# Issuing the loads of x and of the first three weights earlier in the sync engine's order

## The reference, cut to what matters

```
h = max(layernorm(x), 0);  x = x + L0(h, edge_weight, W_gcn, W_mlp)      # 2 rounds: A_norm @ h, @ W_gcn, @ W_mlp, leaky relu
h = max(layernorm(x), 0);  x = x + L1(h, node_vec1, ...)                 # 4 blocks of attention over edges and an MLP
h = max(layernorm(x), 0);  x = x + L2(h, W, b, diffusion_weights)        # 3 steps of adj @ cur
h = max(layernorm(x), 0);  x = x + L3(h, edge_type, basis, att, ...)     # 2 relational layers
                           # in L3: w[r] = sum_b att[r, b] * basis[b], basis is 30 x 512 x 512 per layer
```

## Time and profile before

| what | value |
|---|---|
| median of three runs | 956.01 us |
| the profiled execution | 957.61 us, of which the span from first to last instruction is 955.9 us |
| PE busy | 868.6 us (91%) |
| DVE busy | 547.2 us (57%) |
| ACT busy | 425.0 us (44%) |
| DMA, over the span | 113.27 MB, mean 118 GB/s |
| granted TensorE clock, mean | 0.957 |

### The profile page before, as it was taken

One profiled execution on the slowest core, in us unless ns is written; L12 is line 12 of the kernel. 1 busy time (PEld: TensorE's weight loads), 2 busy tenths in 40 slices (PEclk: granted clock), 3 DMA queues, 4 the chain that ended last, 5 costly groups with the idle time before them and its releaser, 6 DMA issues.

```text
span 955.9 us, 14568 instructions
## 1 busy us (share of the span) xinstructions
PE 868.6 (91%) x4318; PEld 665.3 (70%) x4319; DVE 547.2 (57%) x1212; ACT 425.0 (44%) x700; POOL 224.7 (24%) x245
## 2 busy tenths in 40 slices
PE   6999799987799998999999999999998883999998
PEld 3665565665578786787867878777876562877877
DVE  7999978566654566445674546745476657310210
ACT  4999863242247533476234762237721242030210
POOL 4000052053502235122242223341143043022200
PEclk9999999997799999999999999999999797699799
DMA  8999535433534445344462535533364660020100
GB/s 186 207 216 291 132 85 138 138 90 113 135 88 123 127 123 157 83 106 139 117 188 53 131 111 150 154 85 102 123 172 155 161 167 13 1 88 1 45 11 34
DMA packets 37801, 113.27 MB, mean 118 GB/s; under 512 B 5892, under 2 KB 6424, under 8 KB 30076
## 3 DMA queue, kind: packets, MB, share of 16 engines
q1 hardware_dynamic: 20572, 79.02, 34.4%
q10 hardware_dynamic: 17184, 33.69, 10.3%
HBM read 105.35 MB, written 7.34 MB: 118 GB/s over the span
## 4 chain that ended last, share of the span: by engine, by line
PE 43%; issue 32%; POOL 12%; DVE 9%; ACT 2%; DMA 1%; SPq 0%; DVEq 0%; POOLq 0%; ACTq 0%
PE ring L1630 25%; POOL wl L669 11%; PE ring L1732 7%; PE ring L1899 5%; PE mix_ps L1750 2%; PE ring L1648 1%; POOL rstd L674 1%; DVE stats L1087 1%; PE mix_ps L1659 1%; PE ring L1709 1%; DMA att<-in_L_gnn_att 1%; DVE y L1096 0%; DVE hb_l L1074 0%; DVE diag L1328 0%; PE ring L1807 0%
## 5 line engine op out<-in xcount | busy, mean ns | idle before, releaser
L669 POOL TENSOR_TENSOR wl<-wraw,wh 128x512 fp32r<-128x512 f32 x140 | 177.4, 1301 | 410.2 <-ACT wh L737 390.6
L1732 PE MATMUL ring<-ohs,ohd 128*128 128x512 f32 x312 | 80.1, 410 | 6.6 <-DVE ohs L1262 6.5
L1732 PEld LDWEIGHTS ring<-ohs,ohd 128*128 128x128 f32 x312 | 59.3, 195 | 31.5 <-issue 18.7
L1240 DVE SCALAR_TENSOR_TENSOR ohd<-iota,dstT,vals 128x256 fp32r x156 | 69.8, 482 | 6.0 <-issue 3.6
L737 ACT ACTIVATE wh<-wraw 128x2048 fp32r<-128x2048 f32 x35 | 66.7, 1906 | 4.9 <-DMA wraw<-in_L_gnn_root 4.9
L1074 DVE TENSOR_TENSOR qk_l<-ring,qk_h 128x512 fp32r<-128x512 f32 x32 | 21.8, 690 | 76.6 <-ACT qk_h L762 76.6
L762 ACT ACTIVATE yT_h<-ring 128x512 fp32r<-128x512 f32 x32 | 19.1, 597 | 101.5 <-PE ring L1648 101.5
L786 ACT ACTIVATE ohs<-iota,minus_srcT 128x512 fp32r<-128x512 f32 x78 | 52.3, 713 | 14.1 <-PE ring L1732 7.8
L674 POOL TENSOR_TENSOR rstd<-ve,half 128x1 f32<-128x1 f32 x48 | 27.3, 572 | 109.3 <-DVE ve L1092 109.3
L1659 PE MATMUL mix_ps<-quad,att_shift 120*32 120x512 f32 x384 | 52.2, 629 | 0.0
L1074 DVE TENSOR_TENSOR PT_l<-ring,PT_h 128x512 fp32r<-128x512 f32 x64 | 39.7, 682 | 19.6 <-ACT PT_h L762 19.6
(11 more groups left out here) (373 smaller groups left out, 2238.1 us busy)
## 6 DMA issues: line engine op xcount, KB each, us to landing
quad<-in_L_gnn_basis SPq DMA_DIRECT2D x60, 960.0 KB, 8.5
wraw<-in_L_gnn_m_w ACTq DMA_DIRECT2D x8, 1024.0 KB, 5.1
mix_scratch<-mixed SPq DMA_DIRECT2D x128, 32.0 KB, 3.7
wraw<-in_L_gnn_wv ACTq DMA_DIRECT2D x4, 1024.0 KB, 5.3
wraw<-in_L_gnn_wq ACTq DMA_DIRECT2D x4, 1024.0 KB, 5.2
wraw<-in_L_gnn_wk ACTq DMA_DIRECT2D x4, 1024.0 KB, 5.9
wraw<-in_L_gnn_wo ACTq DMA_DIRECT2D x4, 1024.0 KB, 5.4
wraw<-mix_scratch ACTq DMA_DIRECT2D x4, 1024.0 KB, 5.5
```

Source lines behind the costliest of these rows:

```text
L669: last = g.tensor_tensor(wl[s][:, k, :], wraw[s][:, k, :], wh[s][:, k, :].bitcast(F32), ALU.subtract)
L1240: return v.scalar_tensor_tensor(out, at.unsqueeze(1).broadcast_to([P, 4, HALF]), dstT[:, e], vals[:, e, :].rearrange("p a b -> p (a b)").u ...
L1732: last = te.matmul(ring[:, banks[b], :], ohd[:, s, b, :], ohs[:, s, :], start=False, stop=False)
```

## The change

The load of `x` is issued after group 6 and no longer after group 13. The loads of w0, w1 and w2 are issued after groups 8, 10 and 12 and no longer all three after group 15. Sizes, targets, semaphores and all that the other engines do stay the same.

```
             for g in range(GROUPS, EARLY_SETS * GROUPS):
                 if g < PASS_GROUPS:
                     load_pass_group(g // GROUPS, g % GROUPS)
-                    if g == PASS_GROUPS - 3:
+                    if g == GROUPS + 2:
                         sp.dma_start(x[:], rows(x_d)).then_inc(x_loaded, 16)
-                    elif g == PASS_GROUPS - 1:
-                        for w in range(3):
-                            sp.dma_start(wraw[slot(w)][:], weight_source(w)).then_inc(weight_loaded[slot(w)], 16)
+                    elif g in (8, 10, 12):
+                        w = (g - 8) // 2
+                        sp.dma_start(wraw[slot(w)][:], weight_source(w)).then_inc(weight_loaded[slot(w)], 16)
                 else:
                     load_group(g // GROUPS, g % GROUPS)
                 if g >= 6 and g % GROUPS == 2:
                     store_set(g // GROUPS - 1)
```

## The result

The changed kernel is **slower** by 0.7%: 964.17 us (median of four runs, 962.82 to 965.1) against 956.81 us for the kernel before in the same session (four runs, 955.05 to 957.64). The ratio is 1.0074, with a 95% interval of 1.0054 to 1.0093. The prediction was wrong: 958.1 us with a range to 962.3 us. The time is 1.9 us above the top of that range, and rival B (962.2 us) was nearest.

The account below looks back on a forecast made before the run. PE, DVE and the DMA queue feeding PE's groups were taken to bound the edge pass at almost the same pace. 0 for landings, 0 for issuing and +2.1 us for DVE's lateness on 956.0 gave 958.1 us, range 955.3 to 962.3.

Parts of the forecast that it names:

- rival B: At group 13's wait: the stall of 4.47 us passes whole and the clock falls, 1.7 us; 962.2 us, chance 0.23.
- Earlier landings: At the first readers of `x` and the weights: landing sooner saves nothing, since `x` is already 21 us early; 0 us.
- PE's waits at line 1750: In the edge pass: PE waits for basis groups near 74 and 87 us, some 4.5 us in all.
- DVE's at line 1246: At the move of the half: DVE waits for PE, and the statistics of `x` start at 101.5 instead of 99.45 us.
- PE's idle time before the restart: After the 32 units, before the next one-hots: PE's gap shrinks from 5.2 to about 3 us.
- what each load costs in the queue: In the DMA queue of the basis groups: the four moved loads delay group 13 by 11.87 us together.
- the upper bound of 19.7 us: In the DMA queue: the four loads' sum if each costs as much as a group in the new places.
- the range of PE's lateness: After group 13: PE is 4.5 us late, with bounds of 3.4 and 12.3 us.
- DVE's room: At the half moved at 87.04 us: 2.40 us of PE's 4.47 us are absorbed, so DVE is 2.1 us late.
- the clock: At PE's restart and after stalls: nothing booked; up to 1.7 us gained at the restart or lost inside the loop.
- the prediction's own sign: At the statistics of `x`: a start over 4 us late would show that the stall passes whole and the clock falls.
- the prediction's service in order of issue: In the busy DMA queue: DMAs are served in order of issue, so the distance between landings is a load's service time.

Follow-up runs that it names:

- e1: Against the changed kernel, only the load of `x` stays early, the three weights go back behind group 15: 956.64 us, before 956.87.
- e4: The changed kernel, but groups 4 to 15 load only one of their four rows, 240 KB instead of 960 KB: 956.83 us, before 956.87.
- e8: The changed kernel, but `x` and the weights are loaded in pieces of 8 KB instead of 2 KB: 964.84 us, ratio 1.0085.
- e2: Against the changed kernel, `x` goes back behind group 13, the weights stay behind groups 8, 10 and 12: 960.77 us, ratio 1.004.
- e6: Against the changed kernel, w1 and w2 go back behind group 15, `x` and w0 stay early: 959.8 us, ratio 1.0038.
- e7: Against the changed kernel, only w2 goes back behind group 15, `x`, w0 and w1 stay early: 964.15 us, ratio 1.0078.
- e3: Against the changed kernel, all three weights are issued in a row behind group 8, `x` stays behind group 6: 965.39 us, ratio 1.009.
- e5: Against the changed kernel, ACT issues all four loads on its own queue before the edge pass, SP none: 968.47 us, ratio 1.0129.
- e10: Against the changed kernel, POOL instead of DVE computes the statistics of `x`; `x` is behind group 13, weights behind 15: 963.06 us, ratio 1.0061.
- e9: Against the kernel before, POOL instead of DVE computes the statistics of `x`; `x` is behind group 6, weights behind 15: 962.02 us, ratio 1.0055.

## Why the prediction was wrong

**Held.** Earlier landings save nothing (e1). The price is the groups' delay in the full queue (e4), it shows as PE's waits at line 1750 and DVE's at line 1246, and it ends with the statistics of `x`: the stages behind kept their length to 0.3 us. PE's idle time before the restart shrank from 5.23 to 3.67 us, where about 2.8 or 3 was given. The chain of the prediction was right; the sizes of its terms were not.

**Failed: what each load costs in the queue.** The sum took 2.77, 2.65, 2.71 and 3.74 us, 11.87 us together. The delay of group 13 is 16.1 us, about 4 us for a load. This is the largest error. The four prices were read from landings at one place of the kernel before and did not carry to the new places. Why they are higher there stays open. Piece size is excluded (e8). That the loads stand between groups isn't enough (2.5 us each in e2). Bytes at the mean rate of the queue would fit the change: the window of 30 to 95 us before has 241 GB/s, and an estimate from it is 4.35 us for 1024 KB, 17.4 us for four. It doesn't fit e2. The prediction had the upper bound of 19.7 us (each load like a group) and used it for the range of PE's lateness only.

The groups 7 and 9 stall, which the prediction never looked at: it began at group 11. By its own prices it would have found no stall there: 2.77 us against a margin of 5.2 us at group 7, and 2.77 + 2.65 = 5.42 us against 61.62 - 56.0 = 5.6 us at group 9. With the measured delays, 5.5 and 8.6 us, both are late.

The Trainium skill ("DMA: Bandwidth & Descriptors", section "Why a DMA increments its semaphore by 16 and not by 1") says that a DMA is spread over the largest number of engines up to 16 that divides the slowest dimension of both sides. By that rule a group of 30 matrices by 4 rows, on 120 partitions, would go over 15 engines and a load on 128 partitions over 16, both with 64 KB for each. An estimate from it is that a load costs as much as a group, 4.9 us; the 4.4 and 4.8 us behind groups 8 and 12 are close to it, the 2.4 to 3.1 us in e2 are not. No run here shows the bytes of a single engine, so this stays open.

**Failed: DVE's room.** The prediction put `half_ready` 0.6 us behind the start of the zero matmuls and got 2.40 us of room. Where DVE really waits, its move starts 1.35 us behind that start: at 80.67 against 79.32 us in the change, and by 1.36 us in e2 and e8. At the lower clock it is 1.92 us (94.77 against 92.85 us). So the room at the half behind group 13 was 87.04 - 84.04 - 1.35 = 1.65 us. Behind group 9 it was less still:

```profile
62.62 1.20 PE L1709 MATMUL ring<-zero_l 128*128 128x512 f32 x4
```
```profile
64.68 0.68 DVE L1246 COPY Csum<-ring 64x512 f32 x1
```

That is 2.06 - 1.35 = 0.7 us. In e6 the zeros started 3.55 us later than before and signalled 0.6 us later again at the lower clock; less 0.7 us of room this gives 3.4 us, and DVE's move was 3.40 us late (68.08 against 64.68). In e2 the room did cover a stall: the zeros behind group 15 started 1.88 us late and DVE's move 0.23 us late.

**Failed: the clock.** It was booked at nothing, with up to 1.7 us as a remark. The stalls of 2.65 and 2.78 us were each followed by 3.4 us at 1.2 GHz, which cost PE 1.4 to 1.5 us each inside the loop. The stalls of 1.54 and 1.43 us were not. It is not strict: in e7 a stall of 2.79 us passed without a fall, and one of 3.19 us brought 6.8 us at 0.58 of full clock.

**The sum with what was measured.** Group 13 lands 16.1 us late, less its margin of 7.4: PE uses it 8.7 us late (4.47 was given), and its zeros start 8.8 us late. `half_ready` comes 0.6 us later at the lower clock, and the room covers 1.65 us. So DVE's move is 94.77 - 87.04 = 7.7 us late, and with 0.61 us of waiting for a slot the statistics are 8.3 us late, as measured. The stalls at groups 7, 9 and 11 are no further terms: they bring forward a part of the same lateness.

By the prediction's own sign (the statistics over 4 us late) it was rival B, but B's number was near partly by luck. B has the clock fall after a stall, and so it was. B also has no room at the half, and the room was there, only smaller; and it took the queue's delay from the same 11.87 us.

## What to carry to other kernels

Before a load is moved ahead in a full queue, list every consumer behind it with its own slack, the nearest first, and don't take the load's price from one other place in the queue: the same 1 MB loads cost a group 2.5 us each in e2, 3.4 in e3 and 4 in the change. A stall of the matrix engine is priced with the stretch at the lower clock that may follow, and the room of the engine that follows it is read at each place where it waits, with the signal's delay taken from a wait that a trace shows. A landing that is 21 us early is worth nothing earlier, and an issue moved to a busy engine can hold that engine.

## What the runs showed of the hardware

- **An issue can hold its engine.** ACT's fourth 1 MB load in a row took 11.09 us to issue, where the three ahead of it took 0.4 to 0.5 us each (e5). SP's issue of w2 took 0.61 us before, 2.73 us in the change, and in e3:

```profile
41.53 8.93 SPq L542 DMA_DIRECT2D wraw<-in_L_gnn_W_gcn  x1
```

- **A later DMA can delay an earlier one of the same queue.** Group 6 is issued before `x` both times, yet with `x` behind it, it lands 16.5 us after its issue at 26.56 us, at 43.1; before, 13.3 us after its issue at 27.88 us, at 41.2. In the runs without `x` behind it (before, e2, e10) it lands 2.5 to 2.7 us after group 5, in those with it (the change, e1, e3, e6 to e9) 3.4 to 4.4 us. The Trainium skill ("DMA: Bandwidth & Descriptors", section "Queues, rings and completion order") says that each DMA engine takes up its descriptors in ring order, that a later one may still finish its write before an earlier one, and that completion is not first in, first out for the issuing engine. These landings agree with it; the prediction's service in order of issue does not.
- **POOL slows DVE.** In e9 the one-hots take 798 and 810 ns beside POOL against 477 and 479 ns without it. The Trainium skill ("GPSIMD Engine Reference", section "Key points") says that POOL shares its SBUF interfaces with VectorE, with contention for instructions with two SBUF inputs or in a mode that uses two ports. The sign agrees for `ohd`, which reads two tensors in SBUF; whether `ohs`, which reads one, falls under that rule no run shows. The size here is 1.7 times for both.
